# Attention and experts on one core: three of four chunks of probabilities turned by VectorE blocks and SBUF transfers, products with V taken in the next step

## The reference, cut to what matters

```python
# x (32, 256, 512), context (32, 256, 512); 16 heads of 32; one mask (256, 256)
def attention(q, k, v, mask, wq, bq, wk, bk, wv, bv, wo, bo):
    qh, kh, vh = proj(q, wq, bq), proj(k, wk, bk), proj(v, wv, bv)   # heads of 32
    scores = einsum('bhqd,bhkd->bhqk', qh, kh) / sqrt(32)
    scores = where(mask, scores, -1e9)
    out = einsum('bhqk,bhkd->bhqd', softmax(scores), vh)
    return out.reshape(b, s, d) @ wo.T + bo

x = x + attention(layernorm(x), context, context, mask, ...)
x = x + experts(layernorm(x))    # 8 experts, top 2 of each token, capacity 2048, silu(a) * g
```

## Time and profile before

| | |
|---|---|
| time, median of 3 runs | 2905.82 us (2905.27 to 2906.19) |
| the profiled execution's own time | 2904.62 us |
| its span, first to last instruction | 2902.8 us |
| mean granted TensorE clock | 0.986 |
| busy share TensorE, VectorE, ScalarE, GpSimd | 96%, 54%, 48%, 44% |

### The profile page before, as it was taken

The page is one execution under the profiler, slowest core; times in us unless marked ns, Lnnn a source line. Parts: engine busy times, 40 slices in busy tenths (PEclk is TensorE's granted clock), DMA queues, the critical chain, the costliest instruction groups (busy, mean ns, idle before and its releaser), DMA issues.

```text
span 2902.8 us, 53377 instructions
## 1 busy us (share of the span) xinstructions
PE 2795.4 (96%) x17696; PEld 2295.8 (79%) x17696; DVE 1560.2 (54%) x5034; ACT 1400.3 (48%) x3686; POOL 1270.3 (44%) x1917
## 2 busy tenths in 40 slices
PE   6999999999999999938999999999999999999998
PEld 5888888888888888726888888888888888888886
DVE  5788888888888888834333242332332332423331
ACT  5777777777777777723233232232332322323321
POOL 5677777777777777641122222222121212121211
PEclk9999999999999999968999999999999999999999
DMA  4343344444334344335343443434343434343312
GB/s 149 96 112 112 110 118 111 115 112 118 109 100 113 111 112 118 93 95 133 90 91 91 84 99 81 101 81 95 87 95 78 105 77 95 85 86 93 74 30 29
DMA packets 217032, 281.64 MB, mean 97 GB/s; under 512 B 38720, under 2 KB 128832, under 8 KB 215232
## 3 DMA queue, kind: packets, MB, share of 16 engines
q1 hardware_dynamic: 153696, 144.89, 19.2%
q0 software_dynamic: 32768, 67.26, 12.8%
q10 hardware_dynamic: 30304, 66.07, 6.7%
HBM read 109.53 MB, written 67.90 MB: 61 GB/s over the span
## 4 chain that ended last, share of the span: by engine, by line
PE 54%; DMA 1%; SPq 0%; issue 0%; POOL 0%; DVE 0%; ACT 0%; POOLq 0%
PE a_ps L1427 18%; PE g_ps L1427 18%; PE y_ps L1442 18%; DMA out<-y,recs 0%; SPq L1220 0%; DMA xg<-xn_rows,gather_ids 0%; POOL xg L1266 0%; DMA lists<-table 0%; DMA x_quarters<-xg 0%; DVE xe_lo L1361 0%; POOL out L1294 0%; ACT xe_hi L1321 0%; DVE x_turned L1374 0%; ACT y L1354 0%; DVE act_part L1374 0%
## 5 line engine op out<-in xcount | busy, mean ns | idle before, releaser
L1294 POOL DMA_INDIRECT out<-y,recs x128 | 205.7, 1607 | 1186.5 <-ACT y L1354 840.5
L384 POOL TENSOR_SCALAR probs<-probs,row_inv 128x256 f32<-128x256 f32 x1024 | 502.2, 507 | 267.2 <-DVE row_inv L661 261.2
L483 ACT ACTIVATE probs<-probs,low 128x256 f32<-128x256 f32 x1024 | 511.0, 502 | 188.2 <-DVE low L652 165.8
L1401 DVE TENSOR_TENSOR hidden<-act_part,g_ps 128x512 f32<-128x512 f32 x192 | 132.1, 688 | 858.9 <-ACT act_part L1340 858.9
L652 DVE CUSTOM_DVE_ANT_0 probs<-scores_ps,mask_add,row_any 128x256 f32<-128x256 f32 x1024 | 429.0, 474 | 28.8 <-PE scores_ps L969 28.8
L1427 PE MATMUL a_ps<-xe_hi,fc_hi 128*128 128x512 f32 x768 | 300.2, 391 | 39.8 <-DVE xe_lo L1361 39.8
L1427 PE MATMUL a_ps<-xe_lo,fc_hi 128*128 128x512 f32 x768 | 299.8, 390 | 0.0
L1427 PE MATMUL a_ps<-xe_hi,fc_lo 128*128 128x512 f32 x768 | 299.7, 390 | 0.0
L1427 PE MATMUL g_ps<-xe_hi,fc_hi 128*128 128x512 f32 x768 | 299.0, 389 | 0.0
L1427 PE MATMUL g_ps<-xe_lo,fc_hi 128*128 128x512 f32 x768 | 298.8, 389 | 0.0
L1442 PE MATMUL y_ps<-pj_hi,ht_lo 128*128 128x512 f32 x768 | 298.8, 389 | 0.0
(11 more groups left out here) (172 smaller groups left out, 6510.3 us busy)
## 6 DMA issues: line engine op xcount, KB each, us to landing
probs_m<-blocks SPq DMA_DIRECT2D x1024, 64.0 KB
x_quarters<-xg SPq DMA_DIRECT2D x512, 64.0 KB, 2.0
fc_raw<-in_c_fc SPq DMA_DIRECT2D x24, 1024.0 KB, 5.7
out<-x_xn ACTq DMA_DIRECT2D x32, 512.0 KB, 2.8
xn_rows<-x_xn ACTq DMA_DIRECT2D x32, 512.0 KB, 4.9
cin<-in_ctx_t ACTq DMA_DIRECT2D x31, 512.0 KB, 5.8
xin<-in_x ACTq DMA_DIRECT2D x31, 512.0 KB, 4.3
pj_raw<-in_c_proj SPq DMA_DIRECT2D x8, 1536.0 KB, 6.6
```

The lines of the kernel that those rows point to most:

```text
L384: last = nc.gpsimd.tensor_scalar(probs[:, r, t, :], probs[:, r, t, :], row_inv[:, r, t:t + 1], 1.0, ALU.mult, ALU.mult)
L483: last = nc.scalar.activation(probs[:, r, t, :], probs[:, r, t, :], ACT.Exp, scale=-1.0, bias=low[:, r, t:t + 1], accum_out=row_sum[:, r, ...
L1294: nc.gpsimd.indirect_dma_start(out=out[:, :], out_offset=bass.IndirectOffsetOnAxis(ap=recs[:, i * CT + t, 0:1].bitcast(U32), axis=0), in_= ...
L1401: nc.vector.tensor_tensor(hidden[:, m % 2, :], act_part[:, m % 2, :], g_ps[m % 2][:, :], ALU.mult).then_inc(gated, 1)
```

## The change

Chunks 0, 1 and 2 of a step are now transposed by VectorE's blocks and SyncE's transfers, and chunk 3 alone by TensorE and ScalarE. `probs_m` has two halves, used in turn, and `moved` is a semaphore for each group `a`, so that `turn(g, a)` waits for the transfers of its own group only. `move_of(g)` counts the moves, three a step. `move` waits for the product with V of the chunk two moves back, whose half it takes. All four products of an element stand in the step after its own: chunks 0 and 1 right behind the first scores, chunks 2 and 3 where they were, ahead of the second. VectorE turns chunk 1 in two parts, ahead of and behind the masks of chunk 2, and chunk 2 ahead of and behind those of chunk 3. No amount of arithmetic changes.

```diff
--- before.py
+++ after.py
@@ -51,6 +51,7 @@
 PASSES = ((0, 0), (0, 1), (1, 0))
 HALVES = 2
 W_ORDER = (1, 0, 2, 3)
+MOVES = 3
 
 def need(eng, sem, value):
 
@@ -122,7 +123,7 @@
 
         blocks = sb("blocks", [P, GROUPS, HPC * TILES * TILES * DK])
 
-        probs_m = sb("probs_m", [P, GROUPS, HPC * TILES * TILES * DK])
+        probs_m = sb("probs_m", [P, 2, GROUPS, HPC * TILES * TILES * DK])
 
         probs_t = sb("probs_t", [P, HPC, TILES, SEQ])
         low = sb("low", [P, RING, TILES])
@@ -198,7 +199,7 @@
         inverted = sem("inverted")
         normed = sem("normed")
         turned = sem("turned")
-        moved = sem("moved")
+        moved = [sem(f"moved{a}") for a in range(GROUPS)]
         pe_turned = sem("pe_turned")
         pe_copied = sem("pe_copied")
         attended = sem("attended")
@@ -239,6 +240,11 @@
 
             return 0 <= n < BATCH
 
+        def move_of(g):
+
+
+            return g // DC * MOVES + g % DC
+
         def load_c(eng, b):
 
             need(eng, ct_split, b * DC)
@@ -261,14 +267,16 @@
 
                 def move(g):
 
-
-                    need(sp, attended, g - 1)
+                    i = move_of(g)
+                    if i >= 2:
+
+                        sp.wait_ge(attended, (i - 2) // MOVES * DC + (i - 2) % MOVES + 1)
                     for a in range(GROUPS):
                         settle(sp)
-                        sp.wait_ge(turned, g // 2 * GROUPS + a + 1)
+                        sp.wait_ge(turned, i * GROUPS + a + 1)
                         for j in range(GROUPS):
-                            sp.dma_start(probs_m[a * DK:(a + 1) * DK, j, :],
-                                         blocks[j * DK:(j + 1) * DK, a, :]).then_inc(moved, 16)
+                            sp.dma_start(probs_m[a * DK:(a + 1) * DK, i % 2, j, :],
+                                         blocks[j * DK:(j + 1) * DK, a, :]).then_inc(moved[a], 16)
 
                 load_x(sp, 0)
                 load_c(sp, 0)
@@ -291,8 +299,9 @@
 
                 sp.wait_ge(w_split, 1)
                 load_w(3)
-                for g in range(0, BATCH * DC, 2):
-                    move(g)
+                for g in range(BATCH * DC):
+                    if g % DC < MOVES:
+                        move(g)
                 sp.wait_ge(defaults_stored, 16 * (EXPERTS + 2))
                 sp.wait_ge(x2_stored, 16 * BATCH)
                 sp.wait_ge(xn2_stored, 16 * BATCH)
@@ -459,10 +468,10 @@
                     nc.scalar.copy(v[:, b % 2, t, :], (bank_b, bank_c)[t][:, :]).then_inc(v_ready, 1)
 
                 def turned_out(g, r):
-                    act.wait_ge(pe_turned, g // 2 * HPC + r + 1)
+                    act.wait_ge(pe_turned, g // DC * HPC + r + 1)
                     if r == 0:
 
-                        need(act, attended, g - 1)
+                        need(act, attended, g - DC + 1)
                     nc.scalar.copy(probs_t[:, r, :, :], scores_ps[r][:, :, :]).then_inc(pe_copied, 1)
 
                 def attn_hi(g):
@@ -497,6 +506,8 @@
                     if heads:
                         exponents(h)
                     if tail:
+                        attn_hi(g - 4)
+                        attn_hi(g - 3)
                         turned_out(g - 1, 0)
                     if late:
                         act.wait_ge(xn2_ready, n - 1)
@@ -549,16 +560,12 @@
                             exponents(h + 2 * HPC + r)
                         if r == 1 and proj and n >= 0:
                             x_hi(n + 1, 1)
-                        if heads:
-                            turned_out(g + 1, r)
 
                     if tail:
                         act.wait_ge(x2_ready, n * TILES)
                         settle(act)
                         act.dma_start(out_rows[n - 1], x2).then_inc(x2_stored, 16)
                     if heads:
-                        attn_hi(g)
-                        attn_hi(g + 1)
                         exponents(h + 3 * HPC)
                         exponents(h + 3 * HPC + 1)
                     if late:
@@ -643,10 +650,10 @@
                     dve.wait_ge(scored, g // HPC + 1)
 
                     chunk = g // HPC - 2
-                    if chunk % 2:
-                        need(dve, pe_turned, chunk // 2 * HPC + g % HPC + 1)
-                    else:
-                        need(dve, turned, (chunk // 2 + 1) * GROUPS)
+                    if chunk % DC == DC - 1:
+                        need(dve, pe_turned, chunk // DC * HPC + g % HPC + 1)
+                    elif chunk >= 0:
+                        dve.wait_ge(turned, (move_of(chunk) + 1) * GROUPS)
                     settle(dve)
                     for t in range(TILES):
                         last = nc.vector.tensor_tensor_reduce(
@@ -663,9 +670,8 @@
                 def turn(g, a):
 
                     dve.wait_ge(normed, (g + 1) * HPC)
-                    if a == 0:
-
-                        need(dve, moved, QUARTERED * (g // 2))
+
+                    need(dve, moved[a], 16 * GROUPS * move_of(g))
                     of = probs[:, g % 2 * HPC:g % 2 * HPC + HPC, :, :].rearrange("p h t k -> p (h t k)").rearrange(
                         "p (b a l) -> p b a l", a=GROUPS, l=DK)
                     nc.vector.transpose(blocks[:, a, :].rearrange("p (b l) -> p b l", l=DK),
@@ -801,6 +807,9 @@
 
                     if heads:
                         scores(g)
+                    if tail:
+                        attn_lo(g - 4)
+                        attn_lo(g - 3)
                     if proj and n >= 0:
                         moments_x(n + 1)
                     if heads:
@@ -829,7 +838,11 @@
                         invert(g * HPC + HPC + 3)
 
                     if heads:
+                        turn(g + 1, 0)
+                        turn(g + 1, 1)
                         scores(g + 2)
+                        turn(g + 1, 2)
+                        turn(g + 1, 3)
                     if proj and n >= 0:
                         x_lo(n + 1, 1)
                     if tail:
@@ -844,14 +857,14 @@
                         x2_out(n - 1, 1)
 
                     if heads:
-                        for a in range(GROUPS):
-                            turn(g + 2, a)
+                        turn(g + 2, 0)
+                        turn(g + 2, 1)
                         scores(g + 3)
+                        turn(g + 2, 2)
+                        turn(g + 2, 3)
                     if tail:
                         moments_x2(n - 1)
                     if heads:
-                        attn_lo(g)
-                        attn_lo(g + 1)
                         invert(g * HPC + 3 * HPC + 2)
                     if late:
                         place_out(n - 2)
@@ -938,13 +951,16 @@
                 def attend(g):
 
                     b, c = divmod(g, DC)
-                    if g % 2:
-                        pe.wait_ge(pe_copied, (g // 2 + 1) * HPC)
+                    if c == MOVES:
+                        pe.wait_ge(pe_copied, (b + 1) * HPC)
                         of = probs_t[:, :, :, :]
                     else:
-                        pe.wait_ge(moved, QUARTERED * (g // 2 + 1))
+                        for a in range(GROUPS):
+                            pe.wait_ge(moved[a], 16 * GROUPS * (move_of(g) + 1))
+                        of = probs_m[:, move_of(g) % 2].rearrange("p j (h t u l) -> p h u t j l", h=HPC, t=TILES,
+                                                                  u=TILES)
+                    if c % 2 == 0:
                         need(pe, at_split, g)
-                        of = probs_m[:, :, :].rearrange("p j (h t u l) -> p h u t j l", h=HPC, t=TILES, u=TILES)
                     if c == 0:
                         pe.wait_ge(v_ready, (b + 1) * TILES)
                     for u in range(TILES):
@@ -960,9 +976,9 @@
                     pe.wait_ge(q_ready, g + 1)
                     pe.wait_ge(k_ready, g + 1)
                     need(pe, masked, g * HPC)
-                    if g % 2:
-
-                        need(pe, pe_copied, g // 2 * HPC)
+                    if c == 1:
+
+                        need(pe, pe_copied, b * HPC)
                     for t in range(TILES):
                         for r in range(HPC):
                             rows_of = slice(r * DK, (r + 1) * DK)
@@ -1063,6 +1079,10 @@
 
                     if heads:
                         score(g)
+                    if tail:
+                        attend(g - 4)
+                        attend(g - 3)
+                    if heads:
                         values(n, 0, 0)
                     if tail:
                         probs_turn(g - 1, 0)
@@ -1108,12 +1128,8 @@
                         for half in range(HALVES):
                             if tail:
                                 outputs(n - 1, t, half)
-                            if heads:
-                                probs_turn(g + 1, t * HALVES + half)
-
```

(5 more changed lines are left out.)

## The result

| | before | after |
|---|---|---|
| median | 2905.55 us (2903.95 to 2906.19) | 3095.93 us (3091.67 to 3098.16) |
| ratio to before | | 1.0655, 95% interval 1.064 to 1.0671 |
| span of the profiled execution | 2902.8 us | 3093.7 us |
| mean granted TensorE clock | 0.986 | 0.957 |

The account below looks back on a forecast made before the run. TensorE's work and a ring through five queues were taken to bound the 38.15 us step jointly. The ring grows to 43.0 us, 150 us in all; with 40 for the clock, 2904.6 becomes 3095 (forecast 3096), range 2970 to 3140.

Parts of the forecast that it names:

- Two bounds at once in the kernel before: Attention half: TensorE's work and a ring through five queues both bound the 38.15 us step; shortening TensorE's work alone gains nothing.
- The products with V move onto the ring: Products of chunks 0 and 1, now between first and second scores, lengthen that stretch from 12.06 to 13.92 us.
- the ring: Dependent work through five queues from one step's first scores to the next's: 38.15 us before, 43.0 forecast.
- The doubled buffer does not free the third move: Chunk 2's transfers wait for chunk 0's product in the next step; first to second scores take 16.4 us, not 13.92.
- the 77 that 2.5 us a step made: Forecast cost of TensorE's wait ahead of chunk 2's product: first to second scores 16.4 us instead of 13.92.
- the 2.0 us of landing: Time for chunk 2's transfers to land after issue, taken from a like transfer in the expert half; bounds 1 and 3.
- Chunk 1's transposes ahead of the third masks: VectorE's two transposes before the third chunk's masks: second scores to those masks take 10.66 us in place of 9.17.
- The stretch behind them: Third chunk's masks to the last reciprocal on VectorE: two more transposes partly fill idle times, 7.98 us instead of 7.75.
- Clock: TensorE's gap at the step's end halves its clock for scores and first product: 2.0 us in two steps of three, 40 us.
- The gap at the end: TensorE's idle time at the end of a step, ahead of the next first scores: 4.2 us forecast.
- VectorE comes to the second scores before TensorE has made them: Between first and second scores, VectorE's work stays covered by TensorE's, so it adds nothing to the 13.92 us there.
- The rival with the hidden move: Chunk 2's move delays nothing: a step of 40.5 us, 2.37 more, about 2979 us; chance 0.12.

Follow-up runs that it names:

- the early copy: The kernel before, with ScalarE's copy of the first half of the queries two heads earlier in its queue: 2904.49 us, ratio 0.9999.
- the kernel with one gap filled: The changed kernel, with 11 unread matmuls on TensorE at each step's end, ahead of the first scores: 3093.69 us, ratio 1.0647.
- the kernel with both repairs: The changed kernel, with chunk 0's product back in its own step and ScalarE's copy of the queries ahead of the last exponentials: 2992.3 us, ratio 1.03.
- the two filled runs with chunk 0's product in its own step: The changed kernel with that product moved back and 16 unread matmuls in TensorE's gap: 2970.81 us; with queries also copied early: 2967.76 us.

## Why the prediction was right

It gave 3096 us, and the median is 3095.93. That close a match owes something to luck: single terms were off by some 25 us, in both directions, as the split below shows.

- *Two bounds at once in the kernel before.* Shown. Moving two products with no change of work costs 49 us; removing one wait in the early copy brings up the next.
- *The products with V move onto the ring:* 1.86 us a step, 58 us forecast, 49 measured by the kernel that does this alone.
- *The doubled buffer does not free the third move.* SyncE's wait, the 12.28 us from issue to product (12.3 forecast), and the vanishing of TensorE's wait with chunk 0's product in its own step show it. With the clock up in both, the kernel with chunk 0's product late takes 3047.5 and that with it in its own step 2970.8, 77 us apart. If one product is half of the 49, which no run isolates, the hold is some 52 us, under the 77 that 2.5 us a step made. The wait itself was not smaller than forecast, 3.06 us at the full clock in the kernel with one gap filled: freeing the move is worth less than the wait, since VectorE is next. For the 2.0 us of landing, taken from another transfer, the page of the kernel with both repairs has this transfer's own median, 2.5.
- *Chunk 1's transposes ahead of the third masks:* 10.72 for 10.66. The stretch behind them was over-sized, 7.21 for 7.98: the four transposes and the idle times they fill overlap better than I allowed.
- *Clock:* 48 us, with 40 forecast (1.3 us a step, 2.0 in two steps of three). This is a near hit of two errors: the clock fell in 21 steps of 22, and the scores and the two products behind them took up to 5.6 us for 2.9, more than the 2.0 allowed. A mean of 0.93 over 1100 us is 154 us at the lower level, some 6.2 us a step and so 3.1 us of lost work; about half of that did not reach the time, since 48 us are 1.5 a step; that the held move and the waits behind it hid it is argued, not shown. The Trainium skill (TensorE: Matmul & The Clock Gate, "Why this matters for your kernels") warns of gaps between bursts; the trace agrees in 21 of the 22 gaps of about 3 us ahead of the first scores, and not in the one at 463.38. The gap at the end was forecast at 4.2 us and is 3.1; 0.8 of the difference is the stretch that took 7.21 us and not 7.98.
- *VectorE's queue as a bound of its own* is the step that the forecast lacked. It was taken as covered ("VectorE comes to the second scores before TensorE has made them"), which is true while the move is held and false once it isn't. It costs nothing in the changed kernel, where VectorE waits for the scores, so the forecast was right without it. The rival with the hidden move, 2979, has no run of its own: none has both products late and the move free. The missing bound made the expectations of the two filled runs with chunk 0's product in its own step too low by 41 and 33 us.

A split of the 190 us from these runs: 49 for the late products, 48 for the clock, some 52 for the held move, and the remaining 41 for what the third chunk by blocks costs on the ring and in VectorE's queue, where the forecast's terms for the third chunk make 16 (1.49 + 0.23 - 1.21 us a step). The 41 is a remainder and rests on the halving of the 49. The parts overlap, as the filled gap showed, so this is one order of taking them away and not a sum of independent costs.

## What to carry to other kernels

Before giving work of the busiest engine to another, follow the ring from one step's first instruction to the next one's through every queue: TensorE was 99% busy in a step, but the ring was as long as its work, and none of the ten versions that took 1.6 us from it came under the kernel before. A doubled buffer frees a writer only if the reader of the older half comes first; count which read each half waits for and where in the step that read now stands. And a gap of 3 us in TensorE can cost more than itself, so a kernel that is held elsewhere may pay twice; filling one gap is no test, as the clock may fall in the next.

## What the runs showed of the hardware

Unread matmuls in both gaps took the mean clock from 0.93 to 1.00 and the kernel from 3096 to 3048 us, so work without use can pay. Filling the gap ahead of the first scores alone gave nothing: the clock halved behind the gap left, 3.06 us, instead. Waits of 2.20 us were enough for it too in the kernel with both repairs, where the gap of 2.54 us in the earlier trace rows had left the clock at 1.00. One kernel shows both: with chunk 0's product in its own step, after a gap of 2.55 us, the scores and the product behind them took 1.62 and 1.86 us at 600.73, and 1.08 and 1.00 at 762.89. So the length of a gap alone does not say whether the clock falls.
